# FiLM and the residual sum of layer 0: from VectorE's loop to GpSimd, behind that layer's last gather

## The chip, the cores and the metric

One NeuronCore of one Trainium2 chip runs the whole program. The metric is the device time of one execution in microseconds (us), the median over the runs taken. VectorE is called DVE below, GpSimd POOL, TensorE PE, ScalarE ACT, and SyncE, which issues most of the DMAs, SP.

## The reference

Four graph layers on 6,250 nodes of 128 features and 106,250 edges sorted by target node, all in float32. Each layer normalises X into h and adds its result to X. The change is in the first one (attention over the edges of a node), whose end reads:

```
h = jnp.maximum(_layernorm(x, axis=-1), 0.0)
x = x + _L0_gnn_ref(h, ...)
...
    h_agg = segment_sum(m * attn[..., None], dst).reshape(N, H * Dh)
    out = typed_linear(h_agg, ntype, Wa)
    out = out * alpha + h * (1.0 - alpha)
    out = layer_norm(out, ln_g, ln_b)
    out = out + h
    gamma, beta = split(global_context @ film_w + film_b)
    return gamma[None, :] * out + beta[None, :]
```

So x becomes x + gamma * h + (gamma * ln_b + beta) + gamma * ln_g * normalised. The first three of these terms are known before any edge is worked on. That part, X plus gamma H plus the combined beta, is what the change moves.

## The kernel before, in words

The program is written engine by engine, with semaphores between them. X and H are held in SBUF as 128 partitions x 50 slots (NS) x 128 features. The edges are cut into 896 tiles of 128, four tiles to a quad, 224 quads (NQ); 880 tiles have edges.

Layer 0 is one software pipeline, `layer0_steps`, that every engine walks in the same order: iterations i of 8 quads (u = 0 to 7), 28 of them, and behind them, three iterations late (LAG), the message half of the same quads. So the loop has a head in which there are only scores (i = 0 to 2), a long body, and a tail of three iterations with messages alone.

- Scores, per quad: POOL issues four indirect DMAs (`pool_gathers`, L691), one per tile, that fetch 128 rows of K and V into the ring buffer G of four quads. It may reuse a slot when DVE has multiplied the quad four back and SP has stored the V half to `mvd`. DVE multiplies K by the spread queries (L1770, one input in SBUF, one in PSUM) and reduces (L1787), which counts up the semaphore `reduced`.
- Messages, per quad: DVE builds a one-hot (L1381), weighs the values read back (L1777, both inputs in SBUF: MV and the probabilities in SCR), PE adds by tile, and DVE adds four PSUM rows to the accumulator (L1398), which counts up `rows_added`.
- Every second iteration from i = 3 on DVE runs `maxima` (scans for the softmax maxima, L1706 to L1732, most with two SBUF inputs) and, later in it, `rescale` (L1740 to L1753).
- `film(u)` (L1675 to L1682) runs on DVE at the end of each of the eight steps of iteration 1: seven slots of X and H at a time (PIECE = 7; the eighth piece has one slot), three instructions each: gamma times H into MV, plus beta, and the sum into X. MV is free there, since messages begin in iteration 3.
- `breaks(u)` (L1684 on) runs on DVE in iteration 2.

Behind its last gather POOL waits until all rows are added and puts REL into another order (L733, L735). DVE then runs the output projection (`dve_proj(dve, 1)`), the row moments (`spread()`, L1411 on) and adds the normalised part to X.

Of the kernel before, what the change touches and what calls it, by code (L numbers as in the profile page):

```python
# [8 lines left out]
ALU = mybir.AluOpType  # L9
# [3 lines left out]
P = 128  # L13
D = 128
# [11 lines left out]
PIECE = 7  # L26
# [44 lines left out]
def build(nc, sz, a):  # L71
    NB, NS, T = sz.blocks, sz.slots, sz.tiles
    NQ, PARTS = sz.quads, sz.parts
    LIVE = sz.live
    ctx = ExitStack()
    with ctx:
        def sb(name, shape, dt=F32):
            return ctx.enter_context(nc.sbuf_tensor(name, shape, dt))

        def sem(name):  # L80
            return ctx.enter_context(nc.semaphore(name))
# [15 lines left out]
        X = sb("X", [P, NS, D])  # L97
        H = sb("H", [P, NS, D])
# [5 lines left out]
        MV = sb("MV", [P, RING, QUAD, D])  # L104
        G = sb("G", [P, RING * QUAD * 2 * D])
        SCR = sb("SCR", [P, 3072])
# [6 lines left out]
        ROWS = sb("ROWS", [P, 5, D])  # L113
# [222 lines left out]
        def bc(ap, shape, dim):  # L336
            return ap.unsqueeze(dim).to_broadcast(shape)
# [32 lines left out]
        hop_out = sem("hop_out")  # L370
        exp_in = sem("exp_in")
        exp_out = sem("exp_out")
        w_free = sem("w_free")
        w_next = sem("w_next")
        hist_in = sem("hist_in")
# [221 lines left out]
        scored = {k: sem(k + "_scores") for k in ("far_known", "st_made", "q_spread", "multiplied", "reduced", "grp_turned", "grp_copied")}  # L597
# [73 lines left out]
        def ordered(v):  # L671

            return v.rearrange("o (m g t) -> o m t g", m=PARTS, t=GROUP)
# [22 lines left out]
        @block.gpsimd  # L696
        def _(pool):
            nc.gpsimd.memset(ident[:, :], 0.0).then_inc(consts, 1)
            pool.wait_ge(consts, 1)
            nc.gpsimd.affine_select(out=ident[:, :], in_=ident[:, :], compare_op=ALU.not_equal, fill=1.0,  # L700
                                    base=0, pattern=[[-1, P]], channel_multiplier=1)
            nc.gpsimd.iota(iotaI, pattern=[[1, P]], base=0, channel_multiplier=0)
            nc.gpsimd.iota(pI, pattern=[[0, 1]], base=0, channel_multiplier=1)
            nc.gpsimd.iota(cI, pattern=[[8, NC]], base=0, channel_multiplier=0).then_inc(c_ready, 1)

            pool.wait_ge(row_known, 1)
            nc.gpsimd.indirect_dma_start(
                out=DSTI, out_offset=None, in_=a["dst_pm"],
                in_offset=bass.IndirectOffsetOnAxis(ap=row_i[:, 0:1], axis=0)).then_inc(dst_loaded, 16)

            pool.wait_ge(planned, WINDOWS_KNOWN)
            pool.sem_inc(may_go, 1)
            for c in range(NC):
                for src, dst in ((a["src_win"], SRCW), (a["dst_win"], DSTW)):
                    nc.gpsimd.indirect_dma_start(
                        out=dst[:, c, :], out_offset=None, in_=src,
                        in_offset=bass.IndirectOffsetOnAxis(ap=wI[:, c:c + 1], axis=0)).then_inc(windows_in, 16)

            pool.wait_ge(tiles_stored, STORES)
            starts = flagd.rearrange("t g e -> t (g e)").rearrange("t (m j) -> t m j", m=PARTS)  # L720
            with nc.allow_non_contiguous_dma(reason="single flags"):
                for h in range(HEADS):
                    nc.gpsimd.dma_start(flags[h:P:HEADS, :, 0:sz.span], starts).then_inc(flags_in, 16)
                    nc.gpsimd.dma_start(flags[h:P - HEADS:HEADS, :, sz.span:sz.span + 1], starts[1:GROUP, :, 0:1]).then_inc(flags_in, 16)
                run = sz.chunk * GROUP
                if PARTS > 1:
                    nc.gpsimd.dma_start(LASTK[0:1, 1:PARTS], metad[2:3, run - 1:(PARTS - 1) * run:run]).then_inc(flags_in, 16)
            nc.gpsimd.memset(ACCR[:, :], 0.0).then_inc(acc_cleared, 1)
            for r in range(2):
                pool.wait_ge(proj[0]["stored"][r], 16 * NS // 2)  # L730
            pool_gathers(pool, 0, G2, tab2)
            pool.wait_ge(ps[1]["rows_added"], T)
            nc.gpsimd.tensor_copy(SCR[:, 0:T].rearrange("p (m t g) -> p m t g", m=PARTS, t=GROUP), ordered(REL[:, :])).then_inc(reordered, 1)  # L733
            pool.wait_ge(reordered, 1)
            nc.gpsimd.tensor_copy(REL[:, :], SCR[:, 0:T]).then_inc(reordered, 1)  # L735
            pool.wait_ge(table_out, 48)
            pool_gathers(pool, 2, G1, tab1)

            pool.wait_ge(mixed_out, 16 * TURNS_ALL)
            pool_gathers(pool, 3, G2, tab2)  # L740
            pool.wait_ge(rows_stored, 16 * TURNS_ALL)
            pool_gathers(pool, 4, G1, tab1)
# [628 lines left out]
        def _(dve):  # L1371
            c = Chain(dve, dve_done)
            v_ = nc.vector
# [298 lines left out]
            c(v_.memset(TOP, 2 * NEG))  # L1672
            c(v_.memset(BRK, 2 * NEG))

            def film(u):  # L1675

                some = slice(u * PIECE, min((u + 1) * PIECE, NS))
                wide = [P, some.stop - some.start, D]
                part = MV[:, :, :, :].rearrange("p r j d -> p (r j) d")[:, 0:wide[1], :]
                c(v_.tensor_tensor(part, H[:, some, :], bc(ROWS[:, 3, :], wide, 1), ALU.mult))  # L1680
                c(v_.tensor_tensor(part, part, bc(ROWS[:, 2, :], wide, 1), ALU.add))
                c(v_.tensor_tensor(X[:, some, :], X[:, some, :], part, ALU.add))  # L1682

            def breaks(u):  # L1684

                if u == 0:
# [68 lines left out]
            def step(i, u, scores, messages):  # L1755
                q, slot, turn, v = at(i - LAG, u, -4)
                add = row_adder(1, acc0, WMW, q, v % 2, messages)
                add(0)
                qm, mslot, mturn, mv = at(i - LAG, u, -2)
                weigh = messages and valid(qm)  # L1760
                if weigh:
                    onehot(1, qm, 2 + mv % 2)
                add(1)
                q, slot, turn, v = at(i, u, -2)
                score = scores and valid(q)
                if score:
                    dve.wait_ge(s["q_spread"], q + 1)
                    dve.wait_ge(ps[0]["gathered"][slot], gathered_by(q, slot, turn))
                    wait(dve, s["reduced"], q - 1)
                    v_.tensor_tensor(PROD[:, v % 2, :, :], G2[:, slot, :, 0:D], QD[v % 2], ALU.mult).then_inc(s["multiplied"], 1)  # L1770
                add(2)
                if weigh:
                    dve.wait_ge(mv_loaded[mslot], (mturn + 1) * 16)
                    dve.wait_ge(w["prob_put"], qm + 1)
                    wait(dve, ps[1]["agg_done"], qm - 1)
                    probs = AE[:, (mv // 4) % 2, (mv % 4) * 32:(mv % 4) * 32 + 32]
                    v_.tensor_tensor(  # L1777
                        WM[:, mv % 2, :, 0:D].rearrange("p j (h d) -> p j h d", h=HEADS),
                        MV[:, mslot, :, :].rearrange("p j (h d) -> p j h d", h=HEADS),
                        probs.rearrange("p (j h) -> p j h", j=QUAD).unsqueeze(3).to_broadcast([P, QUAD, HEADS, DH]),  # L1780
                        ALU.mult).then_inc(w["weighted"], 1)
                add(3)
                if score:
                    dve.wait_ge(s["multiplied"], q + 1)
                    if v % 4 == 0:
                        wait(dve, s["grp_turned"], group_of(i, u, -2) - 1)
                    v_.tensor_reduce(ABUF[:, (v // 4) % 2, (v % 4) * 32:(v % 4) * 32 + 32].rearrange("p (j h) -> p j h", j=QUAD),  # L1787
                                     PROD[:, v % 2, :, :].rearrange("p j (h d) -> p j h d", h=HEADS), AX.X, ALU.add
                                     ).then_inc(s["reduced"], 1)
                if isinstance(i, int) and i in hooks[1:] and u == 3:  # L1790
                    dve.wait_ge(ps[1]["rows_added"], hooks.index(i) * sz.chunk * GROUP)
                    rescale(hooks.index(i))
                    dve.sem_inc(rescaled, 1)
                if isinstance(i, int) and i == 1 and u * PIECE < NS:
                    film(u)
                if isinstance(i, int) and i == LAG - 1:
                    breaks(u)
            layer0_steps(dve, step, maxima)
# [9 lines left out]
                               bc(INV, [P, NS, TYPES, HEADS], 2), ALU.mult))  # L1808
            dve.wait_ge(w_next, 16)
            dve_proj(dve, 1)  # L1810
            spread()
            normalise(QT, QT, False)
            for some in (slice(ON_ACT[1], NS), slice(0, ON_ACT[1])):
                if some.start == 0:
                    dve.wait_ge(normed, NORMED[2])
                wide = [P, some.stop - some.start, D]
# [186 lines left out]
```

## Time and profile before

| | |
|---|---|
| median of 3 runs | 5039.2 us (5033.28 to 5042.1) |
| the profiled execution: its time, its span | 5043.33 us, 5041.3 us |
| DVE busy | 3090.2 us (61%), 8230 instructions |
| POOL busy | 3399.2 us (67%), 3564 instructions |
| PE busy | 3019.7 us (60%) |
| ACT busy | 1498.2 us (30%) |
| L691, all gathers of the four layers, POOL | x3520, 3360.6 us, 955 ns each |
| chain of waits that ended last | POOL 43%, issue 20%, DMA 15%, DVE 10%, PE 7% |

Busy time is the sum of an engine's instruction records. The chain is followed back from the last instruction to what released it. In the timelines the columns are the start in us from the span's start, the duration, engine, line, operation, output<-inputs with shapes, the count, and in brackets the idle time before it and what ended it. A row of the windows gives the stretch, its length, then the busy time and count of PE, PE's weight loads, DVE, ACT and POOL, and last the granted PE clock as a share, the DMA share and GB/s. A row of groups gives line, engine, operation, shapes and count, then the busy time in us and the mean in ns, then the idle time before them and what ended it. The time is 2.03 us above the span of the same execution.

### The profile page before, as it was taken

How to read it: one execution, taken by the hardware profiler on the slowest of the kernel's cores; microseconds unless marked ns; L12 is line 12 of the kernel's file. 1: busy time of each engine (PE TensorE's matmuls, PEld its weight loads, DVE VectorE, ACT ScalarE, POOL GpSimd, SP SyncE). 2: the span in 40 equal slices, each digit the busy share in tenths (PEclk: the TensorE clock that was granted, in tenths of full speed). 3: DMA queues.
4: the chain of work that ended last, by engine and by line, in shares of the span. 5: the costliest groups of instructions: out<-in, count | busy, mean ns of one | idle time of the engine just before them, and what ended most of it. 6: DMA issues, size and time to landing. Idle time of an engine off the chain costs nothing.

```text
span 5041.3 us, 77470 instructions
## 1 busy us (share of the span) xinstructions
PE 3019.7 (60%) x15685; PEld 2533.8 (50%) x15686; DVE 3090.2 (61%) x8230; ACT 1498.2 (30%) x2837; POOL 3399.2 (67%) x3564
## 2 busy tenths in 40 slices
PE   5645555555563444455555999999996444444443
PEld 3435555454553444444443777777775434433443
DVE  6377777777777666645553777777775444444443
ACT  1123333333312000011112666666663122222222
POOL 1477777777502777777774777777774777777775
PEclk8767777777776555567775999999998555555555
DMA  2568777787811222222225767766766222222224
GB/s 75 107 171 233 226 233 224 226 230 229 209 50 45 53 53 53 53 60 66 65 66 71 189 189 185 188 186 186 187 185 106 56 56 56 56 56 56 56 56 41
DMA packets 536616, 616.11 MB, mean 122 GB/s; under 512 B 98148, under 2 KB 420751, under 8 KB 536432
## 3 DMA queue, kind: packets, MB, share of 16 engines
q0 software_dynamic: 142256, 349.44, 27.5%
q1 hardware_dynamic: 394176, 264.70, 19.8%
q14 instruction: 129, 1.06, 0.1%
q8 instruction: 55, 0.90, 0.1%
HBM read 529.54 MB, written 84.25 MB: 122 GB/s over the span
## 4 chain that ended last, share of the span: by engine, by line
POOL 43%; issue 20%; DMA 15%; DVE 10%; PE 7%; DVEq 2%; ACT 2%; SPq 1%; POOLq 0%; ACTq 0%
POOL G L691 43%; DMA G<-tab,SRC 9%; DMA mvd<-G 3%; DVE ACCR L1398 2%; PE PB L506 2%; PE PSA L902 1%; PE PB L1088 1%; DVEq L650 1%; DMA MV<-mvd 1%; PE PB L499 1%; PE PB L1026 1%; DVE ACCR L1886 1%; DMA tab<-G 1%; DVE FLG L1868 1%; ACT PB L1244 0%
## 5 line engine op out<-in xcount | busy, mean ns | idle before, releaser
L691 POOL DMA_INDIRECT G<-tab,SRC x3520 | 3360.6, 955 | 1374.1 <-issue 1042.1
L1398 DVE TENSOR_TENSOR ACCR<-ACCR,PSA 128x128 f32 (+2 forms) x3536 | 1126.9, 319 | 750.8 <-PE PSA L902 388.8
L902 PE MATMUL PSA<-G,S 128*128 128x128 f32 x3520 | 861.2, 421 | 1153.1 <-DMA G<-tab,SRC 949.2
L902 PEld LDWEIGHTS PSA<-G,S 128*128 128x128 f32 x3520 | 739.7, 311 | 1263.8 <-DVE ACCR L1398 699.7
L1381 DVE TENSOR_TENSOR S<-PB,REL 128x512 f32<-128x512 f32 x884 | 606.0, 686 | 38.3 <-DVE MASK L1450 13.7
L1026 PE MATMUL PB<-QTR,ST 128*128 x1792 | 341.3, 351 | 300.1 <-ACT ST L1207 162.3
L1026 PEld LDWEIGHTS PB<-QTR,ST 128*128 128x128 f32 x1792 | 299.9, 253 | 335.5 <-issue 334.5
L902 PE MATMUL PSA<-FLG,S 128*128 128x256 f32 x1760 | 421.8, 383 | 2.8 <-DVE FLG L1868 2.7
L902 PEld LDWEIGHTS PSA<-FLG,S 128*128 128x128 f32 x1760 | 337.3, 192 | 146.5 <-issue 91.7
L902 PE MATMUL PSA<-SCR,S 128*128 128x137 f32 x1792 | 330.7, 342 | 18.6 <-DVE ACCR L1398 18.6
L902 PEld LDWEIGHTS PSA<-SCR,S 128*128 128x128 f32 x1792 | 307.3, 248 | 23.3 <-DVE SCR L1777 23.3
L1088 PE MATMUL PB<-G,ident 128*128 128x512 f32 x440 | 245.8, 641 | 96.3 <-DMA G<-tab,SRC 86.9
L1204 ACT ACTIVATE S<-S,small 128x512 bf16<-128x512 bf16 x224 | 161.2, 720 | 372.2 <-DMA S<-relt 371.9
L1080 PEld LDWEIGHTS PB<-W,SCR 128*128 128x128 f32 x1760 | 233.1, 193 | 34.8 <-DMA SCR<-in_ea_t 22.5
L1080 PE MATMUL PB<-W,SCR 128*128 128x128 f32 x1760 | 234.1, 276 | 21.8 <-DMA SCR<-in_ea_t 21.8
L1084 PE MATMUL PB<-QTR,ST 128*128 x1760 | 234.0, 276 | 0.0
L1770 DVE TENSOR_TENSOR SCR<-G,PB 128x512 f32<-128x512 f32 x224 | 152.9, 683 | 107.7 <-issue 57.3
L1084 PEld LDWEIGHTS PB<-QTR,ST 128*128 128x128 f32 x1760 | 215.8, 193 | 0.0
L1868 DVE TENSOR_TENSOR FLG<-G,PB 128x512 f32<-128x512 f32 x220 | 149.6, 680 | 102.1 <-ACT PB L1244 98.9
L1920 DVE TENSOR_TENSOR X<-X,SCR 128x128 f32 x57 | 17.2, 302 | 310.9 <-ACT SCR L1283 310.9
L1242 ACT ACTIVATE FLG<-PB 128x512 f32<-128x512 f32 x220 | 130.2, 592 | 254.4 <-PE PB L1088 253.8
L1777 DVE TENSOR_TENSOR SCR<-MV,SCR 128x512 f32<-128x512 f32 x224 | 154.4, 689 | 75.5 <-DMA MV<-mvd 75.3
(317 smaller groups left out, 3693.0 us busy)
## 6 DMA issues: line engine op xcount, KB each, us to landing
mvd<-G SPq DMA_DIRECT2D x224, 256.0 KB, 3.4
MV<-mvd SPq DMA_DIRECT2D x224, 256.0 KB, 5.1
G<-tab,SRC POOLq DMA_INDIRECT x3520, 2.5
SCR<-in_ea_t SPq DMA_DIRECT2D x880, 64.0 KB
S<-relt SPq DMA_DIRECT2D x224, 128.0 KB
SCR<-reld SPq DMA_DIRECT2D x220, 128.0 KB
tab<-SCR SPq DMA_DIRECT2D x57, 128.0 KB, 1.7
tab<-G SPq DMA_DIRECT2D x50, 128.0 KB, 1.7
```

What stands on the lines that cost most here:

```text
L691: nc.gpsimd.indirect_dma_start(out=rows[:, slot, j, :], out_offset=None, in_=table, in_offset=bass.IndirectOffsetOnAxis(ap=SRC[:, k:k + 1] ...
L902: last = nc.tensor.matmul((PSA if banks is None else banks)[:, par, j, 0:width], S[:, slot, j, :], rhs(j), start=True, stop=True)
L1026: last = nc.tensor.matmul(QD[v % 2][:, j, :], ST[:, v % 2, j, :], QT[:, bass.ds(blocks[j], 1), :].rearrange("p o d -> p (o d)"), start=Tru ...
L1080: nc.tensor.matmul(QD[v % 2][:, j, :], EA[:, slot, j, :], W[:, 4 * D:5 * D], start=j == 0, stop=False, skip_group_check=True)
L1084: nc.tensor.matmul(QD[v % 2][:, j, :], ST[:, v % 2, j, :], QT[:, bass.ds(blocks[j], 1), :].rearrange("p o d -> p (o d)"), start=False, sto ...
L1088: nc.tensor.matmul(QD[v % 2], ident[:, :], G2[:, slot, :, 0:D], start=False, stop=True, skip_group_check=True).then_inc(s["pre_done"], 1)
L1204: nc.scalar.activation(far, far, ACT.Square, bias=minus_p).then_inc(s["far_known"], 1)
L1381: return v_.tensor_tensor(S[:, slot, :, :], bc(IOTAP, [P, QUAD, P], 1), REL[:, bass.ds(q * QUAD, QUAD)].unsqueeze(2).to_broadcast([P, QUAD ...
L1398: v_.tensor_tensor(rows, rows, banks[:, par, j, 0:width], ALU.add).then_inc(s["rows_added"], 1)
L1770: v_.tensor_tensor(PROD[:, v % 2, :, :], G2[:, slot, :, 0:D], QD[v % 2], ALU.mult).then_inc(s["multiplied"], 1)
L1777: v_.tensor_tensor(WM[:, mv % 2, :, 0:D].rearrange("p j (h d) -> p j h d", h=HEADS), MV[:, mslot, :, :].rearrange("p j (h d) -> p j h d", ...
L1868: v_.tensor_tensor(RHS[:, v % 2, :, 0:D], G2[:, slot, :, D:2 * D], GATEP, ALU.mult).then_inc(s["multiplied"], 1)
```

## The change

`film` is deleted from DVE's loop. POOL gets the same 24 instructions, from one loop over the pieces, after its last gather of layer 0 and a wait for the last `reduced`; each is followed by a wait for its own completion (`filmed`). The intermediate goes to the start of SCR, which held the products of the scores, instead of to MV. DVE waits for all 24 before the first `spread()` behind the output projection.

```
@@ -729,6 +730,19 @@
             pool_gathers(pool, 0, G2, tab2)
+
+            pool.wait_ge(scored["reduced"], NQ)
+            steps_done = 0
+            for first in range(0, NS, PIECE):
+                some = slice(first, min(first + PIECE, NS))
+                wide = [P, some.stop - some.start, D]
+                part = SCR[:, 0:wide[1] * D].rearrange("p (b d) -> p b d", d=D)
+                for dst, one, other, op in ((part, H[:, some, :], bc(ROWS[:, 3, :], wide, 1), ALU.mult),
+                                            (part, part, bc(ROWS[:, 2, :], wide, 1), ALU.add),
+                                            (X[:, some, :], X[:, some, :], part, ALU.add)):
+                    nc.gpsimd.tensor_tensor(dst, one, other, op).then_inc(filmed, 1)
+                    steps_done += 1
+                    pool.wait_ge(filmed, steps_done)
             pool.wait_ge(ps[1]["rows_added"], T)
@@ -1672,15 +1686,6 @@
-            def film(u):
-
-                some = slice(u * PIECE, min((u + 1) * PIECE, NS))
-                wide = [P, some.stop - some.start, D]
-                part = MV[:, :, :, :].rearrange("p r j d -> p (r j) d")[:, 0:wide[1], :]
-                c(v_.tensor_tensor(part, H[:, some, :], bc(ROWS[:, 3, :], wide, 1), ALU.mult))
-                c(v_.tensor_tensor(part, part, bc(ROWS[:, 2, :], wide, 1), ALU.add))
-                c(v_.tensor_tensor(X[:, some, :], X[:, some, :], part, ALU.add))
@@ -1791,8 +1796,6 @@
-                if isinstance(i, int) and i == 1 and u * PIECE < NS:
-                    film(u)
@@ -1808,6 +1811,7 @@
             dve_proj(dve, 1)
+            dve.wait_ge(filmed, 3 * -(-NS // PIECE))
             spread()
```

The first place is DVE's queue at the end of iteration 1 and the start of iteration 2. Before (L1770 and L1787 are the scores of a quad, L1680 to L1682 the last piece of `film`, L1690 is `breaks`):

```order
L1770 TENSOR_TENSOR SCR<-G,PB 128x512
L1787 TENSOR_REDUCE SCR<-SCR 128x32
L1680 TENSOR_TENSOR MV<-H,ROWS 128x128
L1681 TENSOR_TENSOR MV<-MV,ROWS 128x128
L1682 TENSOR_TENSOR X<-X,MV 128x128
L1770 TENSOR_TENSOR SCR<-G,PB 128x512
L1787 TENSOR_REDUCE SCR<-SCR 128x32
L1690 TENSOR_REDUCE OUTDEG<-FLG 128x1 x4
```

The same place in the changed kernel (L1775 is the former L1770, L1792 the former L1787, L1695 the former L1690):

```order
L1775 TENSOR_TENSOR SCR<-G,PB 128x512
L1792 TENSOR_REDUCE SCR<-SCR 128x32
L1775 TENSOR_TENSOR SCR<-G,PB 128x512
L1792 TENSOR_REDUCE SCR<-SCR 128x32
L1695 TENSOR_REDUCE OUTDEG<-FLG 128x1 x4
```

Between two quads' scores nothing is left; the same three instructions are gone behind each of the eight quads of iteration 1.

The second place is POOL's queue behind the last gather of layer 0. Before:

```order
L691 DMA G<-tab,SRC 128x256 [waits multiplied_scores,mv_stored2]
L691 DMA G<-tab,SRC 128x256 x3
L733 COPY SCR<-REL 128x896 [waits rows_added_messages]
L735 COPY REL<-SCR 128x896 [waits reordered]
L691 DMA G<-tab,SRC 128x128 [waits table_out]
```

And in the changed kernel, first the head of the new work, then its end:

```order
L692 DMA G<-tab,SRC 128x256 [waits multiplied_scores,mv_stored2]
L692 DMA G<-tab,SRC 128x256 x3
L743 TENSOR_TENSOR SCR<-H,ROWS 128x896 [waits reduced_scores]
L743 TENSOR_TENSOR SCR<-SCR,ROWS 128x896 [waits filmed]
L743 TENSOR_TENSOR X<-X,SCR 128x896 [waits filmed]
```

```order
L743 TENSOR_TENSOR SCR<-H,ROWS 128x128 [waits filmed]
L743 TENSOR_TENSOR SCR<-SCR,ROWS 128x128 [waits filmed]
L743 TENSOR_TENSOR X<-X,SCR 128x128 [waits filmed]
L747 COPY SCR<-REL 128x896 [waits rows_added_messages,filmed]
L749 COPY REL<-SCR 128x896 [waits reordered]
```

Twenty-one instructions of 128x896 and three of 128x128, in line behind one another, now stand between the last gather of layer 0 and the reordering copies.

## Rows read from the trace of the kernel before

**Rows 1.** Busy time by windows: film's stretch, the loop's body, its tail

```profile
245.00:285.00 40.00, 15.54 (x61) 13.31 (x62) 33.08 (x39) 10.40 (x17) 31.47 (x29) 0.50 0.61 164
350.00:1371.00 1021.00, 582.01 (x3365) 531.38 (x3366) 772.02 (x1865) 338.13 (x767) 759.98 (x776) 0.76 0.79 225
1386.00:1467.00 81.00, 48.06 (x216) 41.50 (x215) 65.13 (x177) 9.66 (x37) 0.13 (x1) 0.65 0.25 71
```

**Rows 2.** Groups of POOL, 245 to 285 us, then 285 to 325 us

```profile
L691 POOL DMA_INDIRECT G<-tab,SRC x29 | 32.9, 1134 | 8.8 <-issue 8.8
L691 POOL DMA_INDIRECT G<-tab,SRC x33 | 31.2, 946 | 10.1 <-issue 10.1
```

**Rows 3.** Groups of DVE, 245 to 286 us

```profile
L1681 DVE TENSOR_TENSOR MV<-MV,ROWS 128x896 f32<-128x896 f32 (+1 forms) x8 | 8.1, 1008 | 0.3
L1682 DVE TENSOR_TENSOR X<-X,MV 128x896 f32<-128x896 f32 (+1 forms) x8 | 7.9, 992 | 0.3
L1680 DVE TENSOR_TENSOR MV<-H,ROWS 128x896 f32<-128x896 f32 (+1 forms) x8 | 7.8, 981 | 0.0
...
L1770 DVE TENSOR_TENSOR SCR<-G,PB 128x512 f32<-128x512 f32 x7 | 4.8, 686 | 6.1 <-DMA G<-tab,SRC 6.1
```

**Rows 4.** Timeline of POOL: a gather beside film, one beside a scan

```profile
246.63 1.87 POOL L691 DMA_INDIRECT G<-tab,SRC  x1 [0.30 <-issue]
...
339.65 1.79 POOL L691 DMA_INDIRECT G<-tab,SRC  x1 [0.30 <-issue]
```

**Rows 5.** Timeline of DVE at the same two moments

```profile
246.59 1.09 DVE L1681 TENSOR_TENSOR MV<-MV,ROWS 128x896 f32<-128x896 f32 x1
...
339.46 1.23 DVE L1706 TENSOR_TENSOR_SCAN ACCR<-FLG,ACCR 128x512 f32<-128x512 bf16 x1
```

**Rows 6.** Timeline of POOL, behind the last gather of layer 0

```profile
1466.87 1.71 POOL L733 COPY SCR<-REL 128x896 f32<-128x896 f32 x1 [95.24 <-DVE ACCR L1398]
1468.64 0.93 POOL L735 COPY REL<-SCR 128x896 f32<-128x896 f32 x1
```

**Rows 7.** Timeline of DVE: last reduce, an instruction beside L733, spread, its like alone

```profile
1384.89 0.68 DVE L1787 TENSOR_REDUCE SCR<-SCR 128x32 f32<-128x512 f32 x1
...
1467.08 1.55 DVE L1803 TENSOR_SCALAR ALPHA<-DEG 128x50 f32<-128x50 f32 x1
...
1544.04 0.25 DVE L1411 TENSOR_TENSOR st<-ACCR 128x50 f32<-128x50 f32 x1
...
1545.40 0.19 DVE L1416 TENSOR_SCALAR st<-st 128x50 f32<-128x50 f32 x1
```

**Rows 8.** Groups of DVE in the tail, 1385.6 to 1466.7 us

```profile
L1398 DVE TENSOR_TENSOR ACCR<-ACCR,PSA 128x137 f32 x104 | 30.5, 293 | 12.2 <-DVE ACCR L1398 5.2 <-PE PSA L902 1.6 <-DVE ACCR L1732 0.7
L1777 DVE TENSOR_TENSOR SCR<-MV,SCR 128x512 f32<-128x512 f32 x24 | 16.4, 684 | 0.0
```

**Rows 9.** Timeline of DVE: the last maxima, and two L1777 a step apart

```profile
1400.93 1.22 DVE L1706 TENSOR_TENSOR_SCAN ACCR<-FLG,ACCR 128x512 f32<-128x512 bf16 x1
1402.19 1.22 DVE L1707 TENSOR_TENSOR_SCAN ACCR<-FLG,ACCR 128x512 f32<-128x512 bf16 x1
...
1405.31 0.45 DVE L1712 TENSOR_TENSOR_SCAN ACCR<-ACCR 1x144 f32<-1x144 bf16 x1
...
1406.98 0.16 DVE L1720 TENSOR_TENSOR W<-W,ACCR 1x8 f32<-1x8 f32 x1
1407.18 0.15 DVE L1721 TENSOR_TENSOR W<-W 1x8 f32<-1x8 f32 x1
...
1408.30 1.28 DVE L1728 TENSOR_TENSOR_SCAN ACCR<-FLG,small,ACCR 128x512 f32<-128x512 bf16 x1
...
1410.94 0.69 DVE L1732 TENSOR_TENSOR ACCR<-ACCR 128x512 f32<-128x512 f32 x1
...
1454.15 0.68 DVE L1777 TENSOR_TENSOR SCR<-MV,SCR 128x512 f32<-128x512 f32 x1
...
1456.71 0.68 DVE L1777 TENSOR_TENSOR SCR<-MV,SCR 128x512 f32<-128x512 f32 x1
```

More of the change, by code:

```diff
@@ L372, in build @@
         exp_out = sem("exp_out")
+        filmed = sem("filmed")
         w_free = sem("w_free")
```

## The prediction

> **What bounds the kernel now.** I read the windows first, then the groups of one engine, then the timelines of two engines side by side.
>
> While `film` runs, iteration 1 of layer 0 is POOL's. DVE is busy 33.1 of 40 us and POOL 31.5 [rows 1], which looks like DVE, but busy time misleads here: behind each gather POOL spends 0.30 us on issue [rows 4], so 29 gathers of 1.13 us with that gap take the whole 40 us, and DVE is the one that waits, 6.1 us before its multiplications and each time for a gather [rows 3]. POOL waits for nothing but its own issue there [rows 2]. In the body POOL's 776 gathers and their gaps cover 760 + 233 = 993 of 1021 us [rows 1], so whatever moves POOL's queue early in the layer moves the layer. In the tail, from the last reduction at 1385.6 us [rows 7] to the start of the reordering at 1466.9 [rows 6], it is the other way round: POOL has nothing to do for 95 us [rows 6], and DVE is the chain. It is busy 65 of 81 us, and most of its gaps are waits for its own last instruction or issue [rows 1, 8].
>
> **The gain at the place that loses `film`.** Its 24 instructions take 8.1 + 7.9 + 7.8 = 23.8 us of DVE [rows 3]. That is not the gain, because DVE waits for gathers between them. The gain is what `film` does to POOL. The 29 gathers beside it take 1134 ns in the mean, the 33 behind it 946 ns [rows 2]: 29 x 0.188 = 5.5 us. The timelines show how. A gather that starts at 246.63 takes 1.87 us; DVE's L1681, two inputs in SBUF, runs from 246.59 to 247.68, and the gather ends 0.82 us after it. The one at 339.65 ends about as long after a scan's end [rows 4, 5]. A gather of 0.95 us has 0.13 us behind it when 0.82 are left, so a gather that reads its indices while DVE reads two tensors from SBUF waits for DVE's end. Without `film` POOL keeps its 1.25 us per gather, and everything behind, up to the end of the layer, comes **5.5 us** earlier. I count all of it: the next things that DVE does in iteration 2 (`breaks`) have single inputs, and the gathers beside them run undisturbed [rows 2].
>
> **The cost at the place that receives it.** POOL's wait for the last `reduced` ends at about 1385.6 us. From there it has 81 us until it is needed for the reordering and 158 us until the first spread at 1544.0 [rows 6, 7], where DVE now waits for it. How long 24 POOL instructions take no row shows. Below: a COPY of 128x896, one input, takes 0.93 us; if a second input cost nothing, 21 of these and three short ones give about 21 us. Above: the permuted copy of the same size takes 1.71 us [rows 6]; twice that is 3.4 us, 74 us in all. I take twice the plain copy, 1.9 us, as POOL reads one tensor after the other: 21 x 1.9 + 3 x 0.4 + 23 gaps of 0.06 = 42 us if undisturbed. At none of these values does the wait before `spread` cost anything, nor does anything queue on POOL behind it that is needed sooner: the cover is the output projection, and gone it would be only beyond 158 us.
>
> So the duration does not cost by itself. What may cost is the same port that made the gain, the other way round. Beside L733, a copy that reads SBUF, DVE's L1803 takes 1.55 us, while the like of it alone takes 0.19; it ends at 1468.63, 0.05 us behind L733's end at 1468.58 [rows 6, 7]. A POOL instruction that reads SBUF held that DVE instruction back to its own end. L1803 has one SBUF input, so it is not quite the case in question; the two-input case is shown only in the direction DVE holds POOL. I take it to go both ways. The Trainium skill says so outright (SBUF — State Buffer, Who interferes with whom): a DVE instruction with two SBUF inputs contends with a GpSimd instruction that reads SBUF, and whichever starts first makes the other wait. That rule speaks against this change: by a reading without it the sum would end at the 5.5 us gained, with it the term below comes in. By the same skill (GPSIMD Engine Reference, Performance versus the Vector engine) a two-input addition of 2048 elements takes 4497 ns; scaled, 1.97 us for 896, an estimate from that page that the sum does not use.
>
> Now lay 24 POOL instructions of 1.9 us over DVE's rows of the tail. Each contended DVE instruction lets the next POOL one in when it ends, and waits for it if it comes within 1.9 us.
>
> - The messages: an L1777 every 2.56 us, 0.6 of it its own [rows 9], leaves 1.96 us between two. One POOL instruction just fits, so most waits are near nothing, and a slip costs up to 1.8. About 15 L1777 are met while the work lasts; laid out one by one, five of them wait, 6 us together, and 4 us with the duration or the gap shifted a little. I take 5.
> - The last `maxima`, at 1400.9 [rows 9], falls in the middle: nine instructions with two SBUF inputs (L1706, 1707, 1712, 1713, 1720, 1721, 1728, 1731, 1732). Five of them follow the one before within 0.04 us, as L1721 follows L1720, and wait some 1.85 each, L1720 and L1728 follow at 0.7 and 1.0 us and wait about 1.1 each, L1712 comes 1.9 us later and does not wait, and L1706 waits 1.0 on average. I round 5 x 1.85 + 2.2 + 1.0 = 12.5 down to 12, since releases come some 0.1 us ahead of an end (L1803's own 0.19 us fitted almost wholly before L733's recorded end).
>
> Together 17 us, all on the path, since DVE is the chain there. The POOL work is then done by about 1438 us. L1398, L1381 and the reductions have one SBUF input and go free. SP's and ACT's queues are not touched.
>
> **The sum.** The profiled execution took 5043.3 us; 5043.3 - 5.5 + 17 = 5054.8. The median is 4.1 us lower, so the median of the changed kernel is 5039.2 + 11.5 = **5050.7 us**, +0.23%. Ends: with POOL instructions of 0.93 us the same laying out gives 4 us, so -1.5; with 3.4 us it gives 42, so +37.
>
> **Rivals.** About 0.2% (10 us) is what a measurement of this kernel can tell from no change.
>
> 1. Not slower: the port is one-sided. A POOL instruction holds back only DVE instructions of the kind of L1803, and L1777 and the scans read past it. For it: no row shows a two-input DVE instruction held. Against it: L1803 and rows 4 and 5 are the two halves of one lock. Price: only the gain is left, 5039.2 - 5.5 = 5033.7, -0.11%. It decides from the first L1777 behind the last reduction: if its duration stays 0.68, this is it.
> 2. A short POOL instruction, 1.3 us or so. Then one or two fit between two L1777 and the work is through soon after `maxima`: 10 us by the same laying out, 5044, no change.
> 3. A long one, 2.6 us or more. Then every L1777 waits 0.7 and `maxima` some 17 us: 25 us, 5059; at 3.4 us 5076.
> 4. The gain does not last: POOL comes early to iteration 3 and waits at `maxima` for DVE. Against it, DVE waited for gathers on both sides of `film`. It would give 5056.
> 5. DVE is the bound of iteration 1 after all, and its 23.8 us come back whole, with the tail unhurt: 5015.4. Rows 3, with DVE waiting for gathers, speak against it. That the change does something other than it says I leave out: the order of both queues shows it done.
>
> **How the numbers follow.** Forecast 0.46, rival 1 0.18, rival 2 0.14, rival 3 0.14, rival 4 0.05, rival 5 0.03. The forecast's own range is 5047 to 5055 (the tail's term 13 to 21); about three quarters of it is above +10 us, 0.34. With rivals 3 and 4 slower by over 0.2% has 0.52. Within 0.2% are the rest of the forecast, rival 1, rival 2 and a remainder of 4: 0.45. Faster 0.03. The range 5032 to 5062 takes in the forecast, rivals 1, 2 and 4 and the near half of 3, and leaves out the far half of 3 and rival 5.
>
> **What would show each step.** The gathers of iteration 1 at 0.95 us each, and the last gather 5.5 us earlier, at about 1366: the gain. POOL's 21 long instructions at 1.9 us. L1777 (now L1782) with some rows of 1 to 2.5 us instead of 0.68 just behind the last reduction, the scans of the last `maxima` at about 3 us instead of 1.22, and that `maxima` over 20 us long instead of 10.7: the cost. No wait of DVE at `spread`. The tail from last reduction to reordering 98 us instead of 81. The prediction is wrong if the scans keep their durations, or if the last gather does not move.

## The result, and the profile after

| | before | changed |
|---|---|---|
| median of 6 runs each | 5040.4 us (5033.3 to 5048.3) | 5057.5 us (5053.8 to 5069.1) |
| ratio, 95% interval | | 1.0037 (1.0024 to 1.0051) |
| profiled execution, time and span | 5043.3, 5041.3 | 5057.3, 5055.3 |
| first gather of layer 0 starts | 205.3 us | 206.3 us |
| iteration 1 on POOL, gather 33 to gather 65 | 45.49 us | 40.01 us |
| last gather of layer 0 starts | 1370.7 us | 1365.9 us |
| last reduction starts | 1384.9 us | 1380.8 us |
| the last `maxima` | 10.70 us | 29.42 us |
| the tail: from the last reduction's end to the read of the degrees (DVE, first thing behind the loop) | 81.3 us | 101.1 us |

The change made the kernel slower by 17.1 us in the medians and by 14.0 us between the two profiled executions. From the read of the degrees to the end the two take 3574.5 and 3572.7 us. That difference is not put down to the change, since in the profiles of the last experiments the same stretch takes 3569 to 3578 us, whatever the kernel. One of the 12 runs of the last experiment took 6911 us and counts in no ratio.

**The first place.** The groups of POOL from 245 to 285 us, in the changed kernel:

```profile
L692 POOL DMA_INDIRECT G<-tab,SRC x32 | 30.3, 946 | 9.8 <-issue 9.4 <-DVE SCR L1775 0.3
```

The mean is 946 ns instead of 1134 [rows 2]; all 32 gathers of iteration 1 take at most 0.95 us where seven had taken 1.43 to 1.87, one for each full piece of `film`.

**The tail.** The windows of the changed kernel, film's old stretch and the tail (columns as in [rows 1]):

```profile
245.00:285.00 40.00, 16.99 (x66) 14.46 (x66) 10.98 (x16) 11.25 (x19) 30.26 (x32) 0.50 0.72 184
1381.00:1482.00 101.00, 48.66 (x216) 41.63 (x216) 86.67 (x177) 9.67 (x37) 51.77 (x24) 0.64 0.21 60
```

DVE issues the same 177 instructions in the tail as before and is busy 86.7 us instead of 65.1 [rows 1]. The 21.5 us more are instructions that take longer. I call that a hold: the instruction is on record as running while it waits. Here is the timeline of DVE through the last `maxima` (L1711 is the former L1706, each other line five up likewise):

```profile
1380.76 0.68 DVE L1792 TENSOR_REDUCE SCR<-SCR 128x32 f32<-128x512 f32 x1
...
1382.81 1.35 DVE L1782 TENSOR_TENSOR SCR<-MV,SCR 128x512 f32<-128x512 f32 x1
...
1397.10 2.89 DVE L1711 TENSOR_TENSOR_SCAN ACCR<-FLG,ACCR 128x512 f32<-128x512 bf16 x1
1400.02 2.91 DVE L1712 TENSOR_TENSOR_SCAN ACCR<-FLG,ACCR 128x512 f32<-128x512 bf16 x1
1404.18 0.41 DVE L1714 COPY ACCR<-PB 1x256 f32<-1x256 f32 x1 [1.25 <-PE PB L1023]
1404.63 0.19 DVE L1716 COPY ACCR<-W 1x8 f32<-1x8 f32 x1
1404.85 0.45 DVE L1717 TENSOR_TENSOR_SCAN ACCR<-ACCR 1x144 f32<-1x144 bf16 x1
1405.33 2.14 DVE L1718 TENSOR_TENSOR_SCAN ACCR<-ACCR 1x144 f32<-1x144 bf16 x1
1407.51 4.11 DVE L1720 COPY W<-ACCR 1x128 f32<-1x128 f32 x2
1411.76 1.90 DVE L1725 TENSOR_TENSOR W<-W,ACCR 1x8 f32<-1x8 f32 x1
1413.70 0.15 DVE L1726 TENSOR_TENSOR W<-W 1x8 f32<-1x8 f32 x1
1413.89 0.14 DVE L1727 TENSOR_SCALAR W<-FLG 1x1 f32<-1x1 bf16 x1
1414.06 1.75 DVE L1728 TENSOR_SCALAR W<-W 1x8 f32<-1x8 f32 x1
1415.96 2.00 DVE L1730 COPY W<-ACCR 1x8 f32<-1x8 f32 x1
1417.99 0.16 DVE L1732 COPY small<-PB 128x2 f32<-128x2 f32 x1
1418.19 2.98 DVE L1733 TENSOR_TENSOR_SCAN ACCR<-FLG,small,ACCR 128x512 f32<-128x512 bf16 x1
1421.20 2.91 DVE L1736 TENSOR_TENSOR_SCAN ACCR<-FLG,small,ACCR 128x512 f32<-128x512 bf16 x1
1424.14 2.38 DVE L1737 TENSOR_TENSOR ACCR<-ACCR 128x512 f32<-128x512 f32 x1
...
1428.68 2.48 DVE L1782 TENSOR_TENSOR SCR<-MV,SCR 128x512 f32<-128x512 f32 x1
```

Seven instructions with two SBUF inputs are 1.6 to 1.7 us longer each, 11.8 us together (2.89 - 1.22 for the first [rows 9]). L1717 and L1726 have two SBUF inputs too and go free: each starts 0.02 us ahead of a POOL instruction (below, at 1404.87 and 1413.72). Four one-input instructions from SBUF to SBUF were held as well: the two copies of L1720, L1728 and L1730. These are they in the kernel before:

```profile
1406.27 0.57 DVE L1715 COPY W<-ACCR 1x128 f32<-1x128 f32 x2
...
1407.55 0.22 DVE L1723 TENSOR_SCALAR W<-W 1x8 f32<-1x8 f32 x1
...
1407.91 0.16 DVE L1725 COPY W<-ACCR 1x8 f32<-1x8 f32 x1
```

They lost 6.9 us together. The two copies that read PSUM (L1714, L1732) were not held, nor was L1727, a single bf16 element; why that one goes free was not tried. The many instructions of the tail with one input in SBUF and one in PSUM, L1395 and L1412, keep their 0.68 and 0.29 us beside POOL. The scans read and write FLG and ACCR, which POOL never touches here, so it is not a tile in common that holds them. Of the 24 L1782 two are long, by 0.67 and 1.80 us. The timeline of POOL beside it, its first and five later instructions:

```profile
1381.53 2.08 POOL L743 TENSOR_TENSOR SCR<-H,ROWS 128x896 f32<-128x896 f32 x1 [14.73 <-DVE SCR L1792]
...
1388.74 2.49 POOL L743 TENSOR_TENSOR SCR<-H,ROWS 128x896 f32<-128x896 f32 x1
...
1398.98 2.87 POOL L743 TENSOR_TENSOR SCR<-SCR,ROWS 128x896 f32<-128x896 f32 x1
...
1404.87 2.30 POOL L743 TENSOR_TENSOR SCR<-H,ROWS 128x896 f32<-128x896 f32 x1
...
1411.57 2.07 POOL L743 TENSOR_TENSOR SCR<-H,ROWS 128x896 f32<-128x896 f32 x1
1413.72 2.07 POOL L743 TENSOR_TENSOR SCR<-SCR,ROWS 128x896 f32<-128x896 f32 x1
...
1434.65 0.45 POOL L743 TENSOR_TENSOR X<-X,SCR 128x128 f32<-128x128 f32 x1
```

Undisturbed a POOL instruction takes 2.07 us; behind an L1782 it takes 2.49, behind a scan 2.87. It waits too. The 24 are done at 1435.1, and DVE's first `spread` instruction, which needs them, starts at 1559.9.

### The profile page after: what moved, and what is told of

It reads as the page before. It is cut to its first block, busy times and chain, and to the rows that moved or that the text cites. A ratio compares the mean times of both kernels' runs of the same rounds, so it can differ in the third digit from the quotient of the medians.

```text
span 5055.3 us, 77463 instructions
## 1 busy us (share of the span) xinstructions
PE 3011.4 (60%) x15685; PEld 2526.0 (50%) x15686; DVE 3087.8 (61%) x8206; ACT 1499.1 (30%) x2837; POOL 3445.3 (68%) x3588
## 3 DMA queue, kind: packets, MB, share of 16 engines
q1 hardware_dynamic: 394176, 264.70, 19.9%
## 4 chain that ended last, share of the span: by engine, by line
POOL 41%; issue 20%; DMA 14%; DVE 12%; PE 8%; DVEq 2%; ACT 2%; SPq 1%; POOLq 0%; ACTq 0%
POOL G L692 41%; DMA G<-tab,SRC 9%; DMA mvd<-G 3%; DVE ACCR L1412 3%; PE PB L507 2%; PE PSA L916 1%; PE PB L1102 1%; DVEq L651 1%; PE PB L1040 1%; PE PB L500 1%; DVE ACCR L1890 1%; DMA tab<-G 1%; DMA tab<-H 1%; SPq L788 1%; DVE FLG L1872 0%
## 5 line engine op out<-in xcount | busy, mean ns | idle before, releaser
L1412 DVE TENSOR_TENSOR ACCR<-ACCR,PSA 128x128 f32 (+2 forms) x3536 | 1128.6, 319 | 739.0 <-PE PSA L916 380.4
L1395 DVE TENSOR_TENSOR S<-PB,REL 128x512 f32<-128x512 f32 x884 | 606.6, 686 | 38.3 <-DVE MASK L1464 13.9
L1102 PE MATMUL PB<-G,ident 128*128 128x512 f32 x440 | 244.6, 638 | 96.6 <-DMA G<-tab,SRC 83.9
L1775 DVE TENSOR_TENSOR SCR<-G,PB 128x512 f32<-128x512 f32 x224 | 153.1, 683 | 150.7 <-issue 75.5
L1782 DVE TENSOR_TENSOR SCR<-MV,SCR 128x512 f32<-128x512 f32 x224 | 156.8, 700 | 57.1 <-DMA MV<-mvd 56.6
```

The lines of the kernel that those rows point to most:

```text
L1102: nc.tensor.matmul(QD[v % 2], ident[:, :], G2[:, slot, :, 0:D], start=False, stop=True, skip_group_check=True).then_inc(s["pre_done"], 1)
L1395: return v_.tensor_tensor(S[:, slot, :, :], bc(IOTAP, [P, QUAD, P], 1), REL[:, bass.ds(q * QUAD, QUAD)].unsqueeze(2).to_broadcast([P, QUAD ...
L1412: v_.tensor_tensor(rows, rows, banks[:, par, j, 0:width], ALU.add).then_inc(s["rows_added"], 1)
L1782: v_.tensor_tensor(WM[:, mv % 2, :, 0:D].rearrange("p j (h d) -> p j h d", h=HEADS), MV[:, mslot, :, :].rearrange("p j (h d) -> p j h d", ...
```

## The experiments

The experiments come in three groups, each with the kernel before run beside them. In the first two groups the kernel before itself took 6276 to 6279 us instead of 5034 to 5040, PE and DVE standing idle for long stretches. The DVE waits with the largest sums between 250 and 1750 us in experiment 1 show it (a row gives who waited for whom, the sum in us, how often, and the longest; what "remote" is the profile does not name):

```profile
DVE ACCR L1398 <- remote: 457.2, 52, 15.5
DVE SCR L1770 <- remote: 66.9, 7, 18.9
DVE ACCR L1709 <- remote: 51.2, 8, 7.7
```

The cause is not known; the third group ran on the same chip as the second, and there the kernel before took 5034 us. The durations of single instructions are the same in all three groups and the length of the tail agrees within 1 us, so I read those from every group, and total times of a few us from the third alone.

**1. Film left out.**

```
-                if isinstance(i, int) and i == 1 and u * PIECE < NS:
-                    film(u)
```

> The kernel before with its film instructions left out and put nowhere else (gamma H and beta are missing from X). It measures the gain of the first place alone. Theory, film costs only what its two-input reads take from POOL's gathers: the gathers of iteration 1 at 0.95 us each, the last reduction 5.5 us earlier (4.1 us in the changed kernel's trace), the time 4 to 6 us below the kernel before. Rival, DVE is the bound of iteration 1: 20 us or more below. Second rival, the head start is lost at the maxima: 0 to 2 us below.

Measured: 6276.0 us against 6278.9, ratio 1.0003 (0.9993 to 1.0013); run once more (below) 1.0006 (0.9995 to 1.0017). The gathers of iteration 1 take at most 0.95 us and the last `maxima` 10.69 us, the tail 80.4. But iteration 1 takes 44.0 us here: POOL stands idle for 4.2 us before the 57th gather, and had waited 7.0 us for DVE before the 33rd. So the total says nothing about the gain. A gain of 20 us would have shown in it, but with POOL idle in iteration 1 this settles the rival of a bound DVE for this slower condition only; experiment 12 settles it at 5034 us.

**2. Film on DVE, by way of PSUM.**

```
-                part = MV[:, :, :, :].rearrange("p r j d -> p (r j) d")[:, 0:wide[1], :]
-                c(v_.tensor_tensor(part, H[:, some, :], bc(ROWS[:, 3, :], wide, 1), ALU.mult))
+                bank = PSA[:, :, :, :].rearrange("p r j d -> p (r j d)")
+                part = bank[:, 0:wide[1] * D].rearrange("p (b d) -> p b d", d=D)
+                gamma = bank[:, 8 * D:9 * D]
+                if u == 0:
+                    c(v_.tensor_copy(gamma, ROWS[:, 3, :]))
+                c(v_.tensor_tensor(part, H[:, some, :], bc(gamma, wide, 1), ALU.mult))
```

> The kernel before with film on DVE at its old place, but gamma and the intermediate kept in PSUM, so that none of its instructions reads two tensors from SBUF. Theory, the shared reading is what stretches the gathers: film still takes 23 to 25 us of DVE, the gathers of iteration 1 stay at 0.95 us, and the time is that of the kernel without film, 4 to 6 us below the kernel before. Rival, DVE's time or film's place in its queue is what delays POOL: the same time as before.

Measured: 6277.5 us, ratio 1.0006 (0.9996 to 1.0016). No gather of iteration 1 is over 0.95 us, with film's instructions of 1.09 to 1.10 us beside them. The total is not resolved; see the third group.

**3. POOL busy, but only writing.**

```
-            for first in range(0, NS, PIECE):
...
+            for r in range(RING):
+                pool.wait_ge(mv_stored[r], NQ // RING * 16)
+            for steps_done in range(1, 3 * -(-NS // PIECE) + 1):
+                nc.gpsimd.memset(G[:, 0:2048], 0.0).then_inc(filmed, 1)
+                pool.wait_ge(filmed, steps_done)
```

> The changed kernel with POOL's 24 film instructions replaced by 24 memsets of 128x2048 floats into a dead part of G, some 1.7 us each, chained in the same way (gamma H and beta are missing from X). POOL is as busy in the tail but reads nothing from SBUF. Theory, what holds DVE is POOL's reading: L1782 keeps 0.68 us and the two-input scans of the last maxima 1.2 us, the tail stays at 81 us, and the time is that of the kernel without film, within 3 us. Copies with one SBUF input might still be held by the writing: then up to 6 us more. Rival, any POOL instruction beside DVE costs: a tail of 95 us or more and a time above the kernel before.

Measured: 6282.2 us, ratio 1.0010 (0.9996 to 1.0024); the tail 87.3 us, the `maxima` 16.55. The group of POOL's memsets, and then part of DVE's timeline in that `maxima` (lines six below those of the changed kernel):

```profile
L738 POOL MEMSET G<- 128x2048 f32 x24 | 43.3, 1806 | 20.3 <-DVE SCR L1786 18.9
```

```profile
1769.03 1.22 DVE L1705 TENSOR_TENSOR_SCAN ACCR<-FLG,ACCR 128x512 f32<-128x512 bf16 x1
1770.28 1.23 DVE L1706 TENSOR_TENSOR_SCAN ACCR<-FLG,ACCR 128x512 f32<-128x512 bf16 x1
...
1772.96 1.58 DVE L1710 COPY ACCR<-W 1x8 f32<-1x8 f32 x1
1774.58 0.45 DVE L1711 TENSOR_TENSOR_SCAN ACCR<-ACCR 1x144 f32<-1x144 bf16 x1
...
1775.54 2.85 DVE L1714 COPY W<-ACCR 1x128 f32<-1x128 f32 x2
...
1780.31 1.72 DVE L1724 COPY W<-ACCR 1x8 f32<-1x8 f32 x1
```

With POOL writing and not reading, every two-input instruction of the tail keeps its time, and all 24 weighings 0.68 or 0.69 us. The one-input copies are held still, and the `maxima` is 5.9 us longer than alone. So there are two holds: POOL's reading holds two-input DVE instructions, and POOL's mere writing already holds one-input copies and tensor-scalar instructions within SBUF. The Trainium skill (SBUF — State Buffer, Who interferes with whom) has both: a DVE instruction with two SBUF inputs contends with a GpSimd instruction that reads SBUF and not with one that only writes, and copies and tensor-scalar operations can enter modes that use two ports and contend with GpSimd. The trace agrees on what is held, with the numbers above; the mode that a copy ran in it does not show.

**4. POOL pauses at the last `maxima`.**

```
             for first in range(0, NS, PIECE):
+                if first == 2 * PIECE:
+                    pool.wait_ge(ps[1]["rows_added"], ((hooks[-1] - LAG) * UNROLL - 4) * QUAD + 1)
```

> The changed kernel with one wait more: after two pieces (six instructions, done before the last maxima) POOL waits until that maxima is over and the first row behind it is added. Theory, 17 to 19 of the 20 us that the tail gained lie in the maxima, where nearly every DVE instruction waits for a POOL one: the maxima takes its 10.7 us again, the L1782 slip a few times and rescale costs up to 3 us, so the tail is 84 to 88 us instead of 101 and the time 12 to 16 us below the changed kernel, about that of the kernel before. Rival, the cost follows the number of POOL instructions wherever they run: the tail stays near 100 us.

Measured: 6285.0 us, ratio 1.0013 (1.0001 to 1.0025). The `maxima` is back at 10.69 us, the tail at 89.0. Of the 8.6 us that are left over experiment 1, two weighings make 1.6 and `rescale`, which now meets POOL, the rest. Part of its timeline, where L1749 took 0.15, L1750 0.27 and L1752 0.16 us when left alone:

```profile
1797.79 1.35 DVE L1749 SCALAR_TENSOR_TENSOR W<-W 1x1 f32<-1x1 f32 x1
1799.17 2.17 DVE L1750 TENSOR_SCALAR W<-iota,W 1x128 f32<-1x128 f32 x1
1801.38 2.06 DVE L1752 TENSOR_SCALAR W<-W 1x8 f32<-1x8 f32 x1
```

So the cost follows what DVE runs beside POOL, not POOL's number of instructions: the same 24 cost the tail 20 us in one place and 9 in the other.

**5 to 8. The second group.** The kernel before took 6276 us. Experiments 5 to 7 are 1, 2 and 4 once more.

> The kernel without film once more, for its total time on a chip where the kernel before takes about 5040 us. Theory: iteration 1 takes 40.0 us of POOL instead of 45.5, nothing else changes, and the time is 4 to 6 us below the kernel before. Rival, the whole of film's 23.8 us comes back: 20 us or more below.

> Film on DVE with gamma and the intermediate in PSUM once more, for its total time. Theory: its instructions take 1.09 us as before but touch no gather, so the time is that of the kernel without film, 4 to 6 us below the kernel before and 20 to 24 below the changed one. Rival, film's time on DVE matters by itself: no faster than before.

> The changed kernel with the pause at the last maxima once more, for its total time. The earlier run showed that maxima back at 10.7 us and the tail at 89 us instead of 101. Theory: the time is 11 to 13 us below the changed kernel, 2 to 5 us above the kernel before. Rival, the tail's loss is made up or given back later: a difference from the changed kernel of under 5 us.

Measured: 6278.7, 6278.5 and 6295.9 us, ratios 1.0006 (0.9995 to 1.0017), 1.0004 (0.9995 to 1.0013) and 1.0029 (1.0018 to 1.0040). The tails are 80.7, 80.1 and 89.0 us, the `maxima` 10.69 us in all three. Iteration 1 of the kernel without film took 46.2 us and not the expected 40.0. The pause cost 6 us the first time and 20 the second with the same tail; the totals of these two groups are not good for less than that.

The new kernel of the group, experiment 8, cuts POOL's work into 150 short instructions, and DVE waits for 150:

```
-            for first in range(0, NS, PIECE):
-                some = slice(first, min(first + PIECE, NS))
+            for first in range(NS):
+                some = slice(first, first + 1)
```

> The changed kernel with POOL's film cut into 150 instructions of one slot (128x128, 0.45 us) instead of 24 of up to seven. POOL reads as much in all and is busy longer, 75 to 85 us, up to the end of the tail. Theory, a held DVE instruction waits for the end of one POOL instruction: the scans of the last maxima at 1.6 to 1.7 us instead of 2.9, that maxima 15 to 18 us instead of 29.4, each of the 24 L1782 up to 0.4 us longer; the tail 88 to 95 us instead of 101, the time 6 to 12 us below the changed kernel. Rival, what counts is how long POOL works beside DVE: a tail of 101 us or more.

Measured: 6277.7 us, ratio 1.0002 (0.9993 to 1.0011), the `maxima` 11.62 us, the tail 82.5. POOL works 96.6 us beside DVE instead of 53.6 and costs the tail about a tenth. The rival, that the length of POOL's work counts, is out; my own estimate of 88 to 95 was too high as well.

**9 to 12. The third group**, at 5034.2 us for the kernel before (24 runs): the changed kernel and the kernel before as they are, then the short pieces and film by PSUM once more.

> The changed kernel itself beside the others, since the chips of the experiments take some 6280 us for the kernel before where the first took 5040. Theory: the tail is DVE's chain on any chip, so the last maxima is 29 us again and the tail 100 to 102 us instead of 80 to 81; iteration 1 is not POOL's here, so nothing is gained there, and the time is 16 to 22 us above the kernel before (0.25 to 0.35%). Rival, the tail has slack on these chips: within 5 us of the kernel before.

> The kernel before, for its profile on such a chip. Theory: film stretches about seven gathers of iteration 1 to 1.4 to 1.9 us here too, but POOL has waits for DVE between them, so iteration 1 is as long as without film (44 to 49 us). Rival, it is 5 us longer than without film, and the gain should be there.

> The pieces of one slot in the same call as the changed kernel. The earlier run had the last maxima at 11.6 us and the tail at 82.5 us. Theory: the time is 15 to 20 us below the changed kernel and within 5 us of the kernel before. Rival, 150 instructions on POOL cost what the 24 cost: within 5 us of the changed kernel.

> Film on DVE by way of PSUM in the same call as the changed kernel. Theory: on a chip where iteration 1 is not bound by POOL it is worth nothing against the kernel before (within 5 us) and 15 to 20 us below the changed kernel; on a chip where it is, 4 to 6 us below the kernel before.

| | time, us | ratio to before | iteration 1 | the last `maxima` | tail |
|---|---|---|---|---|---|
| kernel before | 5034.2 | | 44.97 | 10.70 | 80.9 |
| changed kernel | 5049.8 | 1.0028 (1.0016 to 1.0040) | 40.14 | 29.43 | 101.1 |
| short pieces on POOL | 5032.6 | 0.9998 (0.9989 to 1.0007) | 40.09 | 11.45 | 82.0 |
| film on DVE by PSUM | 5027.5 | 0.9987 (0.9978 to 0.9996) | 39.99 | 10.69 | 80.6 |

The expectations of the first two took for granted that the kernel before needs some 6280 us and that POOL has slack in iteration 1. It took 5034, the rival of the second came true, iteration 1 is 5.0 us longer with film, and the changed kernel is 15.6 us slower, just under the 16 to 22 expected without a gain. The seven stretched gathers are the whole of it, and the two ways to be rid of them, moving film or having it read one input from PSUM, do equally well. The groups of POOL and of DVE in the kernel with film by PSUM, at film's place:

```profile
L691 POOL DMA_INDIRECT G<-tab,SRC x33 | 31.2, 945 | 10.1 <-issue 9.7 <-DVE SCR L1774 0.3
```

```profile
L1685 DVE TENSOR_TENSOR PSA<-PSA,ROWS 128x896 f32<-128x896 f32 (+1 forms) x8 | 8.0, 1000 | 0.3
L1684 DVE TENSOR_TENSOR PSA<-H,PSA 128x896 f32<-128x896 f32 (+1 forms) x8 | 7.9, 986 | 0.0
L1686 DVE TENSOR_TENSOR X<-X,PSA 128x896 f32<-128x896 f32 (+1 forms) x8 | 7.9, 986 | 0.3
```

Film takes the same 23.8 us of DVE as before [rows 3] and the gathers 945 ns instead of 1134. The whole gain of the first place is had without POOL: 6.6 us in the medians (2 to 11 by the interval), by 24 instructions that stay where they were and one copy of gamma of 0.28 us. It is the fastest of all kernels here. The changed kernel has the same iteration 1 and is 22.2 us slower, of which the tail explains 20.5. The short pieces are 5.1 us slower, of which the tail explains 1.4; where the rest lies the profiles do not settle. In the profile of the short pieces, the same instructions of the `maxima`:

```profile
1394.85 1.27 DVE L1711 TENSOR_TENSOR_SCAN ACCR<-FLG,ACCR 128x512 f32<-128x512 bf16 x1
...
1400.21 0.88 DVE L1720 COPY W<-ACCR 1x128 f32<-1x128 f32 x2
...
1402.28 0.30 DVE L1730 COPY W<-ACCR 1x8 f32<-1x8 f32 x1
...
1405.54 0.76 DVE L1737 TENSOR_TENSOR ACCR<-ACCR 128x512 f32<-128x512 f32 x1
```

These are 0.05 to 0.16 us longer each instead of 1.7. How far the 5 us of iteration 1 last cannot be read from single profiles: from the first gather to the last reduction the kernel before takes 1176.7 us here, film by PSUM 1171.1, the short pieces 1175.3 and the changed kernel 1180.4, in an execution that at 5065 us was the longest of its six. The stretch behind iteration 1, where no gather was changed, takes 1077 to 1086 us in these four. The medians have to decide, and film by PSUM has them 6.6 us lower.

## Why the prediction was right, step by step

- **Film's place costs 5.5 us, by its reads and not its 23.8 us.** Right: 45.49 - 40.01 = 5.5 us in iteration 1. Shown twice over in the third group, by taking film away from there (40.1 us) and by leaving it with one input in PSUM (40.0). The rival of a bound DVE is out: film by PSUM keeps all of DVE's time and has the gain. That the gain lasts (rival 4 said no, at 5056) is shown less sharply: measured from the first gather, the last gather is 5.8 us earlier and the last reduction 5.1, film by PSUM has 6.6 us in the medians, but the changed kernel's profile of the third group does not show it. The third group's medians speak for it too: 5034.2 plus 20.2 of tail is 5054.4, less the 5.0 gained 5049.4, and 5049.8 was measured. That the first 5057.5 lies near rival 4's price proves nothing for it, since the tail cost more than that rival reckons.
- **POOL's instruction takes 1.9 us.** It takes 2.07 undisturbed, and the whole sequence 53.6 us (1381.5 to 1435.1) where the prediction had some 52.
- **POOL holds two-input DVE instructions.** Right: the scans take 2.89 us instead of 1.22, so the rival of a one-sided port is out. That it is POOL's reading is shown by the memsets, which read nothing and hold none.
- **Twelve us at the last `maxima`.** The term as it was reckoned, two-input instructions only, measured 11.8. That is partly luck: of the five that follow at once, reckoned at 1.85 us each, four were held 1.7 and one not at all, and the other three were held 1.7 each where 1.0 and 1.1 were reckoned. The step that failed is the limit to two-input instructions: the sentence on L1803 had shown a one-input instruction held, and the count of the `maxima` then left such ones out. They cost 6.9 us more. This is what mis-sized the sum: 18.7 us at that place instead of 12.
- **Five us at the L1777.** Too much: 2.5 us of hold measured, and only 1.1 of it lengthened the tail, as 15.36 us from the last reduction to the `maxima` became 15.66, and 55.21 us behind it became 56.05. At 2.07 us a POOL instruction does not fit into the gap between two L1777 as the prediction had it, but it is POOL that pays: with 0.42 us of waiting it fell into step with the 2.56 us of a quad at once, and five L1782 in a row pay nothing.
- **The sum.** The tail grew by 19.9 us (11.8 + 6.9 + 1.1), not 17: a term that was left out and one that was too large cancelled in part. With the gain of 5.5 that is 14.4, and 14.0 was the difference of the profiled executions. The medians differ by 17.1 and, in the third group, by 15.6; the forecast was 11.5, and 5057.5 us lies above its own range of 5047 to 5055 and inside the full one of 5032 to 5062. Direction, both places and the main mechanism were right, the size a fifth to a third too small.
- **Nothing waits before `spread`.** Right: POOL's work ends 47.6 us before its own next copy, and DVE's first `spread` instruction, 125 us after that end, starts 0.13 us behind the instruction before it.

## What to carry to other kernels

When GpSimd and VectorE run side by side, look at the operands before the durations: an instruction whose inputs both lie in SBUF competed with GpSimd's reads (a scan took 2.89 us instead of 1.22), and a copy or a tensor-scalar operation from SBUF to SBUF competed even with memsets (1.72 instead of 0.16). Putting one operand in PSUM removed the loss for one copy of 0.28 us, where moving the work to the idle engine gained the same 5.5 us and cost 20. If the work must go to GpSimd, cut it small and keep it away from chains of short dependent VectorE instructions, since each link can wait for nearly one whole GpSimd instruction.

## What the runs showed of the hardware that was not expected

- In a chain of VectorE instructions each loses less than the GpSimd instruction takes, by a nearly fixed part. At 2.07 us they waited about 1.7 us, at 1.81 us (the memsets) up to 1.56, at 0.46 us about 0.1: some 0.25 to 0.4 us less each time. For L1712 the rows show where that goes, if POOL works for 2.07 us: POOL's instruction ends at 1401.85, so it began at 1399.78, 0.24 us before L1712 comes at 1400.02; and the last 1.22 us of L1712 begin at 1401.71, 0.14 us before POOL's end. This fits that 150 short instructions cost the tail 1 to 2 us and 24 long ones 20, though the short ones take 1.8 times as long in all.
- A copy of 1x8 elements in one partition waits as long as a scan of 128x512: 2.00 us instead of 0.16.
- The order of the two starts decides whether a gather is held. In iteration 1 of the kernel before, each of the seven long gathers starts 0.04 to 0.47 us behind the start of one of film's instructions and ends 0.82 us after its end. Gathers that start 0.04 to 0.11 us ahead of one take 0.95 us, and so does the one that starts only 0.03 us behind. A held gather sets the next one just ahead of film's next instruction, so that each piece of film holds one gather and not three. POOL first, then DVE, in the kernel before:

```profile
255.92 1.57 POOL L691 DMA_INDIRECT G<-tab,SRC  x1 [0.30 <-issue]
257.80 0.94 POOL L691 DMA_INDIRECT G<-tab,SRC  x1 [0.30 <-issue]
```

```profile
255.59 1.08 DVE L1680 TENSOR_TENSOR MV<-H,ROWS 128x896 f32<-128x896 f32 x1
...
257.84 1.09 DVE L1682 TENSOR_TENSOR X<-X,MV 128x896 f32<-128x896 f32 x1
```

- The same kernel on the same chip took 5034 us in one group of runs and 6276 in another, for a reason that the profiles do not name. That stays open.
